# Low parts of the second norm's sum and output: four subtractions of a step move from GpSimd to VectorE

## What is computed

```python
for i in range(NUM_BLOCKS):                 # 4
    residual = x
    q, k, v = x @ Wq[i] + bq[i], x @ Wk[i] + bk[i], x @ Wv[i] + bv[i]
    Q, K = elu(q) + 1.0, elu(k) + 1.0
    KV, Ksum = einsum('nsh,nsh->nh', K, v), sum(K, axis=1)
    V = Q * KV[:, None, :] * (1.0 / (Q * Ksum[:, None, :] + 1e-06))
    a = gelu(gelu(V @ Wo[i] + bo[i]))
    x = _ln(a + residual, ln1_s[i], ln1_b[i])          # first norm
    residual = x
    f = gelu(gelu(x @ W1[i] + b1[i]) @ W2[i] + b2[i])
    x = _ln(f + residual, ln2_s[i], ln2_b[i])          # second norm
```

## Time and profile before

| | |
|---|---|
| three timed runs | 651.79, 648.50, 651.72 us |
| median | 651.72 us |
| span of the profiled execution | 649.9 us |
| busy, share of the span | TensorE 88%, VectorE 71%, ScalarE 59%, GpSimd 18% |
| one even step (line 648 to line 648, from 150.06 us) | 61.6 us |
| one odd step (from 211.68 us) | 61.4 us |

### The profile page before, as it was taken

One profiled execution on the slowest core, in us unless ns is written; L12 is line 12 of the kernel. 1 busy time (PEld: TensorE's weight loads), 2 busy tenths in 40 slices (PEclk: granted clock), 3 DMA queues, 4 the chain that ended last, 5 costly groups with the idle time before them and its releaser, 6 DMA issues.

```text
span 649.9 us, 7136 instructions
## 1 busy us (share of the span) xinstructions
PE 570.2 (88%) x2436; PEld 358.0 (55%) x2436; DVE 460.4 (71%) x807; ACT 380.4 (59%) x371; POOL 116.6 (18%) x62
## 2 busy tenths in 40 slices
PE   4687989988998899989898988998899989894995
PEld 3345635753674466456645653675366565662554
DVE  6856466886678497758766987579477286989644
ACT  2653774767586747766774777476745348237030
POOL 6200010311021112011300311021110119018000
PEclk9877999999999999999999999999999989997997
DMA  6000100000001000000100000000001010000003
GB/s 210 0 2 0 49 2 0 2 0 1 2 0 49 0 0 0 0 0 0 48 1 0 0 0 0 0 0 0 2 0 66 1 65 2 1 0 2 0 1 129
DMA packets 2756, 10.26 MB, mean 16 GB/s; under 512 B 560, under 2 KB 560, under 8 KB 2480
## 3 DMA queue, kind: packets, MB, share of 16 engines
q1 hardware_dynamic: 2736, 9.99, 4.4%
HBM read 7.90 MB, written 2.10 MB: 15 GB/s over the span
## 4 chain that ended last, share of the span: by engine, by line
PE 49%; DVE 31%; issue 10%; ACT 9%; DMA 0%; DVEq 0%; ACTq 0%; SPq 0%
PE tile L892 13%; PE tile L880 6%; PE tile L899 6%; PE tile L1109 5%; PE tile L957 5%; PE tile L963 4%; PE tile L958 4%; DVE y L712 4%; DVE kk L615 3%; DVE kw L609 3%; DVE a L803 2%; DVE y L624 2%; DVE qw L622 2%; ACT y L348 1%; ACT a L384 1%
## 5 line engine op out<-in xcount | busy, mean ns | idle before, releaser
L957 PE MATMUL tile<-xh,wh 128*128 128x512 f32 x224 | 97.0, 433 | 19.2 <-DVE xh L750 9.5
L984 PE MATMUL tile<-h,w 128*128 128x512 f32 x224 | 101.6, 601 | 4.1 <-ACT a L367 2.0
L290 POOL TENSOR_TENSOR xl<-y,xh 128x1024 fp32r<-128x1024 f32 x16 | 38.1, 2381 | 358.4 <-DVE xh L529 358.4
L963 PE MATMUL tile<-xl,wh 128*128 128x512 f32 x224 | 89.0, 409 | 4.6 <-POOL xl L298 4.6
L958 PE MATMUL tile<-xh,wl 128*128 128x512 f32 x224 | 90.5, 404 | 0.0
L373 ACT ACTIVATE h<-tile,b 128x1024 f32<-128x1024 f32 x64 | 69.5, 1109 | 33.9 <-PE tile L963 33.8
L892 PE MATMUL tile<-sq,slide 128*16 128x128 f32 (+1 forms) x640 | 74.9, 276 | 0.0
L984 PEld LDWEIGHTS tile<-h,w 128*128 128x128 f32 x224 | 40.8, 190 | 56.8 <-issue 48.5
L892 PEld LDWEIGHTS tile<-sq,slide 128*16 128x16 f32 (+1 forms) x640 | 59.6, 95 | 19.3 <-ACT yc L327 5.3
L957 PEld LDWEIGHTS tile<-xh,wh 128*128 128x128 f32 x224 | 43.2, 193 | 44.5 <-issue 14.5
L326 ACT ACTIVATE sq<-tile 128x1024 f32<-128x1024 f32 x40 | 41.3, 1032 | 41.2 <-PE tile L880 37.6
(11 more groups left out here) (138 smaller groups left out, 927.1 us busy)
## 6 DMA issues: line engine op xcount, KB each, us to landing
raw<-layers SPq DMA_DIRECT2D x3, 774.5 KB, 4.2
x<-x_t SPq DMA_DIRECT2D x4, 512.0 KB, 6.7
y<-x_t SPq DMA_DIRECT2D x2, 1024.0 KB, 5.1
out_t<-x SPq DMA_DIRECT2D x4, 512.0 KB, 2.6
raw<-layers SPq DMA_DIRECT2D x1, 512.0 KB, 7.6
raw<-layers SPq DMA_DIRECT2D x1, 256.0 KB, 2.6
sq<-fc_t SPq DMA_DIRECT2D x1, 256.0 KB, 7.1
sq<-proj_t SPq DMA_DIRECT2D x1, 256.0 KB, 7.3
```

The source lines that it names most:

```text
L290: pool.tensor_tensor(xl[:, c], y[:, c], xh[:, c].bitcast(F32), ALU.subtract).then_inc(y_lo["2"], 1)
L957: pe.matmul(dst, wh[:, w0:w0 + P], xh[:, c], start=True, stop=False)
L963: mm = pe.matmul(dst, wh[:, w0:w0 + P], xl[:, c], start=False, stop=True)
L984: mm = pe.matmul(dst, w2[:, j * P:(j + 1) * P], h[:, p, j * PAIR + at:j * PAIR + at + BANK], start=(j == 0), stop=(j == FT - 1))
```

## The change

GpSimd's `low_sums` and `low_parts` are gone. VectorE makes the low part of the sum inside `split_sum`, directly behind the cast, and the low parts of the new x in a new function `second_low`: that of p = 0 ahead of the second norm of p = 1, that of p = 1 directly behind it. The subtractions read and write the same tensors and raise the same semaphores as before. In step 7 and in the tail only the low parts of the sums exist.

```diff
--- before.py
+++ after.py
@@ -282,27 +282,6 @@
                 pool.wait_ge(x_lo["2"], p)
                 pool.tensor_tensor(xl[:, c], x[:, c], xh[:, c].bitcast(F32), ALU.subtract).then_inc(x_lo["2"], 1)
 
-            def low_sums(n, done):
-
-                for p in range(PAIRS_PER_BATCH):
-                    c = cols(n, p)
-                    pool.wait_ge(y_hi["2"], done + p + 1)
-                    pool.tensor_tensor(xl[:, c], y[:, c], xh[:, c].bitcast(F32), ALU.subtract).then_inc(y_lo["2"], 1)
-
-            def low_parts(n, t):
-
-                low_sums(n, 2 * (t - 1))
-                for p in range(PAIRS_PER_BATCH):
-                    pool.wait_ge(x_new["2"], 2 * (t - 1) + p + 1)
-                    pool.wait_ge(x_hi["2"], PAIRS + 2 * (t - 1) + p + 1)
-                    pool.tensor_tensor(xl[:, cols(n, p)], x[:, cols(n, p)], xh[:, cols(n, p)].bitcast(F32),
-                                       ALU.subtract).then_inc(x_lo["2"], 1)
-
-            with pool.Fori(0, LAYERS - 1) as i:
-                low_parts(0, 2 * i + 1)
-                low_parts(1, 2 * i + 2)
-            low_sums(0, 2 * (STEPS - 2))
-            low_sums(1, 2 * (STEPS - 1))
 
             for p in range(PAIRS):
                 pool.wait_ge(h_ready, 2 * FT * STEPS + p * FT + 2)
@@ -527,6 +506,9 @@
 
                 dve.wait_ge(y_ready["2"], done + 1)
                 dve.tensor_copy(xh[:, cols(n, p)], y[:, cols(n, p)]).then_inc(y_hi["2"], 1)
+                dve.wait_ge(y_hi["2"], done + 1)
+                dve.tensor_tensor(xl[:, cols(n, p)], y[:, cols(n, p)], xh[:, cols(n, p)].bitcast(F32),
+                                  ALU.subtract).then_inc(y_lo["2"], 1)
 
             def split_low(k, c):
 
@@ -683,7 +665,16 @@
                     else:
                         if not last:
                             dve.wait_ge(x_hi["2"], PAIRS + m)
+                            second_low(0)
                         normed("2", c, rstd, m + 1, m, scale, shift, None if last else PAIRS + m)
+                        if not last:
+                            second_low(1)
+
+                def second_low(p):
+                    m = 2 * (t - 1) + p
+                    dve.wait_ge(x_new["2"], m + 1)
+                    dve.wait_ge(x_hi["2"], PAIRS + m + 1)
+                    split_low("2", cols(b, p))
 
                 def first_scaled(p, at, width):
 
```

## The result

| | before | after |
|---|---|---|
| timed runs | 648.50, 649.68, 651.72, 651.79 us | 632.43, 632.76, 636.81, 637.08 us |
| median | 650.70 us | 634.78 us |
| span of the profiled execution | 649.9 us | 634.9 us |

The ratio of after to before is 0.9764, 95% interval 0.9728 to 0.9799. Forecast were 636.2 us and a span of 634.4.

A forecast was written before the change was run, and what follows sets the result against it. No engine is full; VectorE is held by GpSimd's subtractions in four places a step, and TensorE waits for it in three. Odd steps 8.70, even 5.28, step 7 0.82, tail 0.73: 15.5 us, so 636.2 us, range 632 to 644.

The forecast's parts named there:

- the long instructions are long by themselves: Rival: GpSimd's leaving gives nothing and the subtractions are only added, 14.5 us slower, 666 us; chance 0.03.
- First place: Sums of line 712, held by GpSimd's subtraction while TensorE waits; claimed 1.01 us earlier in each of steps 1 to 7.
- Second place: Subtraction pushes line 693 and ScalarE's high part 1.19 us later; TensorE, waiting for the square, claimed 0.19 us late.
- the cover: Second place: TensorE's products of p = 0 and centering of the other sequence; without it the place costs 1.19 us.
- Ends of the steps: Even step: copy 561 unheld, 0.75 us earlier; odd step: lines 548 and 609 unheld, 1.89 us earlier; three steps each.
- The free copy: Copy of three columns (561) at an even step's end, taken as 0.16 us instead of 2.34.
- Tail: Line 490 freed from GpSimd's last subtraction, new subtraction delaying its root's start by 0.77: 0.73 us earlier.
- more than forecast: Rival: tail clock stays up, about 1.65 us back, 1.7 more if the 0.57 before 609 hides; 632.9 us, chance 0.14.
- a clock that falls in each step: Rival: TensorE's clock falls in each step, one spell of 1.65 us; 11.6 of 15.5 lost, 647.8 us, chance 0.03.

## Why the prediction was right

**What bounds.** Right. VectorE was held by GpSimd's subtractions, and GpSimd's work alone is enough to hold it (667.5 us with work that nobody reads). The rival by which the long instructions are long by themselves falls with the same run.

**First place.** Sized 1.01, measured 1.1 us a step. The gap is this: back to back, the next instruction starts 0.08 us before the recorded end of the one ahead (subtraction at 151.28, 1.22 long, sum at 152.42), so a subtraction in a row costs 1.14 us and not 1.25.

**Second place.** Called 0.19 us late a step, with 1.19 if the cover is gone. In the kernel after it costs 0.1 to 0.25. But the number was right only in company, and so in part by luck. Done alone it costs 0.95 to 1.15 in an even step, since the late high part moves another subtraction of GpSimd deeper into the root. The prediction asked what waits for the late instruction and not what it will collide with; here that did no harm, since the same change removes the collision.

**Ends of the steps.** Sized 0.94 and 2.08 with the lateness of the second place taken out, measured 1.13 to 1.20 and 2.3. The free copy was 0.16 us, as taken. The 0.08 us for each instruction in a row accounts for a part of the remaining 0.2; the rest isn't split up.

**Tail.** This is the step that failed: "0.73 us earlier", and "what holds VectorE later are the hidden sums of lines 311 and 316, which stay". Where the root isn't held, step 7 and tail gain 1.7 us (191.06 and 191.04), close to the 1.55 worked out (0.82 + 0.73). In the profile of the kernel after they lose 2.7. The hidden sums do stay, but where they fall isn't fixed: they wait for TensorE and ScalarE, and the root for VectorE's own chain, and in the kernel before they met only in the root's last instruction, by 0.2 us. What moved them onto the root is the clock.

**The clock in the tail.** The rival "more than forecast" named the place rightly and got the sign wrong. It put the lower clock's absence at 1.65 us gained. In the kernel after the clock is 1.00 there and TensorE is 1.66 us sooner, but this is what brings GpSimd's sums onto the root, and step 7 and tail take 4.4 us more than where the root isn't held. The idle stretch in front of it is no shorter than before (2.07 us, and 1.96 before), and the same tail shows the lower clock in two other kernels' profiles behind 2.08 (the one without the second place and the one with GpSimd held back). TensorE's wait of 0.68 us for GpSimd's last subtraction, at 522.73 in the kernel before, is gone with the change. Whether this makes the higher clock more frequent stays open, and with it whether the kernel before has runs with a held root too.

**The total** is right, 634.8 against 636.2 us, and partly by luck. The steps gave 2.5 us more than forecast, the first part 1.3 that no term foresaw, and the tail 4.2 less. The rival of a clock that falls in each step was given little chance in the kernel after, rightly, as its steps are even; it does strike kernels that leave the first place as it was.

## What to carry to other kernels

Where VectorE and GpSimd both work on SBUF, read the longest duration of each VectorE line against its median before reading busy shares: an instruction of 0.2 us that takes 2.4 beside GpSimd's costs more than doing GpSimd's work on VectorE. A chain of short dependent instructions is the worst neighbour for a row of long GpSimd instructions, since each link can wait for a whole one; give one of the two a wait that keeps them apart. And look for pairs on these two engines that barely meet: here GpSimd's first sum met the last 0.2 us of the root, and 32 matmuls of TensorE at its higher clock were enough to lay it over the rest. One profile of each kernel isn't enough to put such a loss down to the change; the kernels whose tail is the same code showed it both with and without.

## What the runs showed of the hardware

- The hold works both ways: a GpSimd subtraction that starts 0.13 us behind a VectorE subtraction takes 2.84 us where it takes 1.89 when it isn't held, and VectorE's isn't longer (1.22).
- A GpSimd memset of 1023 columns (0.95 us) holds a VectorE copy (1.30 for 0.42) but not a sum of two SBUF tensors (2.35 for two, as alone).
- An idle stretch of 1.89 us of TensorE was followed by the higher clock in every step from 1 on of the kernel before's profile, and by the lower one in 2 of 7 steps of another kernel's at the same place, where it cost 1.7 us. Behind 0.78 us or less at this place the clock fell in none of 49 steps.
- Five VectorE instructions of 16x128, 0.28 us or less each by themselves, took 2.33 to 2.51 us each beside a row of GpSimd sums of 2.4 us: one got through for each sum.
- GpSimd's subtraction takes 1.89 us on one tensor for both inputs and the output, 2.35 to 2.4 on three different ones.
